# A fused convolution-attention, causal attention and expert block: second-norm transposes placed at the end of their slot, the keys' remainder and the projection placed ahead of the diagonals, the first convolution scores placed ahead in their slot, and the convolution sum in 64-token tiles

## The reference, cut to what matters

```python
# 1. convolution attention (per batch, x is 64 x 256, th and ph are 32 x 256)
f = einsum('ci,cj->ij', th, ph)            # th = Wt x + bt, ph = Wp x + bp
a = softmax(f, axis=-1)
x = Wo (a g) + bo + x                      # g = Wg x + bg
# 2. causal attention, 4 heads of 16
t = tokens(x)                              # 256 x 64
t = t + attn(layernorm(t)) @ W_proj
# 3. mixture of 8 experts, all evaluated
u = layernorm(t)
w = softmax(mean_over_batches(u) @ Wr + br)
y_e = relu(bn(relu(bn(u @ W1_e)) @ W2_e)) @ Wo_e + bo_e
out = t + sum_e w_e * y_e
```

## Time and profile before

| | us |
|---|---|
| median of 3 runs | 104.9 |
| those three runs | 104.9, 105.04, 100.9 |
| the profiled execution | 101.54 |
| its span, first to last instruction | 99.7 |
| busy in the span: PE, DVE, ACT, POOL | 81.4, 44.2, 41.8, 15.9 |
| mean granted TensorE clock in the span | 0.914 of full |

### The profile page before, as it was taken

One profiled execution on the slowest core, in us unless ns is written; L12 is line 12 of the kernel. 1 busy time (PEld: TensorE's weight loads), 2 busy tenths in 40 slices (PEclk: granted clock), 3 DMA queues, 4 the chain that ended last, 5 costly groups with the idle time before them and its releaser, 6 DMA issues.

```text
span 99.7 us, 1342 instructions
## 1 busy us (share of the span) xinstructions
PE 81.4 (82%) x482; PEld 51.6 (52%) x482; DVE 44.2 (44%) x138; ACT 41.8 (42%) x81; POOL 15.9 (16%) x27
## 2 busy tenths in 40 slices
PE   5998798586988897909978098897599899799990
PEld 1376697475566475606755055472344347464350
DVE  1027589867694049250861503804212400409751
ACT  2234623355024717613076030158546675663420
POOL 2000214520282012020400201501310200000000
PEclk9999999999669999997599755569999999999999
DMA  1960000000000000000000000000000000000003
GB/s 35 297 262 2 0 0 0 0 7 0 3 0 0 0 0 7 0 0 0 0 0 0 0 0 0 0 3 0 7 0 0 0 0 0 0 0 7 0 0 105
DMA packets 960, 1.83 MB, mean 18 GB/s; under 512 B 119, under 2 KB 568, under 8 KB 954
## 3 DMA queue, kind: packets, MB, share of 16 engines
q1 hardware_dynamic: 732, 1.54, 4.7%
q10 hardware_dynamic: 222, 0.21, 0.8%
HBM read 1.48 MB, written 0.26 MB: 18 GB/s over the span
## 4 chain that ended last, share of the span: by engine, by line
PE 63%; DVE 13%; issue 9%; ACT 8%; POOL 4%; ACTq 0%; POOLq 0%
PE A L615 21%; PE PR L615 18%; PE M L615 10%; PE Q L615 10%; ACT qk_tmp L374 3%; DVE m L525 3%; DVE ln_xs L512 2%; POOL ln_rs L334 2%; PE Q L635 2%; ACT h L384 2%; ACT p L429 2%; DVE th_s L463 1%; DVE ph_s L463 1%; DVE ln_st L501 1%; POOL diag L291 1%
## 5 line engine op out<-in xcount | busy, mean ns | idle before, releaser
L384 ACT ACTIVATE h<-PR,bn_c,bn_s 128x512 f32<-128x512 f32 (+1 forms) x16 | 10.2, 666 | 5.5 <-PE PR L615 5.2
L291 POOL TENSOR_TENSOR diag<-neg_ident,m 128x256 fp32r<-128x256 f32 (+1 forms) x8 | 6.6, 826 | 28.4 <-DVE m L551 17.9
L334 POOL TENSOR_TENSOR ln_rs<-ln_var,half 128x2 f32<-128x2 f32 x8 | 5.6, 700 | 32.0 <-DVE ln_var L506 32.0
L374 ACT ACTIVATE qk_tmp<-PR 128x512 fp32r<-128x512 f32 x8 | 4.3, 594 | 10.8 <-PE PR L615 10.8
L615 PE MATMUL PR<-h,pack_ffn 128*64 128x256 f32 (+2 forms) x32 | 8.6, 446 | 0.0
L551 DVE TENSOR_REDUCE m<-A 128x4 f32<-128x512 f32 x4 | 2.8, 690 | 12.4 <-PE A L615 12.4
L635 PE MATMUL Q<-pack_ident,ln_xs 128*128 128x128 f32 x8 | 1.9, 327 | 6.8 <-DVE ln_xs L512 6.8
L429 ACT ACTIVATE p<-A 128x512 f32<-128x512 f32 (+1 forms) x8 | 6.0, 808 | 2.9 <-PE A L615 2.9
L512 DVE TENSOR_SCALAR ln_xs<-t,ln_mv,ln_rs 128x128 f32<-128x128 f32 x16 | 5.1, 361 | 4.3 <-POOL ln_rs L334 4.3
L604 DVE TENSOR_TENSOR h<-h,A 128x512 f32<-128x512 f32 x8 | 5.1, 684 | 3.9 <-PE A L615 2.8
L615 PE MATMUL PR<-x2T,pack_ffn 64*128 64x512 f32 (+1 forms) x16 | 6.0, 654 | 0.4 <-ACT h L384 0.3
(11 more groups left out here) (118 smaller groups left out, 148.6 us busy)
## 6 DMA issues: line engine op xcount, KB each, us to landing
pack_ffn<-in_pack_ffn_dram SPq DMA_DIRECT2D x1, 712.0 KB, 6.1
pack_attn<-in_pack_attn_dram SPq DMA_DIRECT2D x1, 276.0 KB, 4.0
out_dram<-o_sb SPq DMA_DIRECT2D x2, 128.0 KB, 1.7
x<-in_x_dram SPq DMA_DIRECT2D x1, 195.0 KB
pack_conv<-in_pack_conv_dram ACTq DMA_DIRECT2D x1, 130.5 KB
pack_ident<-in_pack_ident_dram ACTq DMA_DIRECT2D x1, 70.0 KB, 3.6
x<-in_x_dram SPq DMA_DIRECT2D x1, 65.0 KB
```

Source lines behind the costliest of these rows:

```text
L291: return engine.tensor_tensor(out, neg_ident[:, :].unsqueeze(1).to_broadcast([P, n, P]), m.unsqueeze(2).to_broadcast([P, n, P]), ALU.mult)
L334: pool.tensor_tensor(ln[i]["rs"][b][:, :], ln[i]["var"][b][:, :], half[:, 0:NB], ALU.pow).then_inc(ln[i]["s_pow"], 1)
L374: return act.activation(out, in_, ACT.Copy)
L384: act.activation(out, bank, ACT.Relu, bias=bn_c[:, i, q:q + 1], scale=bn_s[:, i, q:q + 1]).then_inc(relu_ok, 1)
```

## The change

Four edits to the order and one to the form of a product:

1. Step 10 (second norm's transposes on PE, the `x2T` copy on ACT) leaves the head of both lists and stands behind 8.2, 12.1 and 12.2, in the same slot.
2. The keys' remainder is step 5.5 now, one slot later, behind step 7; its ACT copy is step 5.6. On ACT the copy of the values (step 5) now comes ahead of it.
3. Step 9 (projection) stands ahead of 7.1 on PE.
4. Step 1 stands ahead of steps 3 and 0 on PE, and ahead of 3 on DVE (9 and 9.1 move within DVE's list too, without a change of order there, since slot 10 holds nothing else that they pass).
5. Each product of step 3 is made as two, with 64 tokens each, whose results lie on partitions 0 to 63 and 64 to 127.

The table of slots now names each fractional step.

```diff
--- before.py
+++ after.py
@@ -262,7 +262,8 @@
 
         FILL = {"loads": 10, "router": 2}
         CONV_STEPS = 4
-        ATTN_SLOT = {4: 4, 5: 5, 6: 7, 7: 8, 8: 9, 9: 10, 10: 11}
+        ATTN_SLOT = {4: 4, 5: 5, 5.1: 5, 5.2: 5, 5.5: 6, 5.6: 6, 6: 7, 6.1: 7, 6.2: 7, 7: 8, 7.1: 8, 8: 9, 8.1: 9, 8.2: 9, 9: 10,
+                     9.1: 10, 10: 11}
         FFN_SLOT = {11.0: 13, 11.1: 14, 12.0: 15, 12.1: 15, 12.2: 15, 12.3: 16,
                     13.0: 16, 13.1: 16, 14.0: 16, 14.1: 16, 14.2: 17, 14.3: 17}
         FFN_PIECES = {11.0: (0, 0, (0, 1)), 11.1: (0, 0, (2, 3)),
@@ -276,7 +277,7 @@
                 return FFN_SLOT[step] if b == 0 else None
             if step < CONV_STEPS:
                 return int(step) + b
-            return ATTN_SLOT[int(step)] + 2 * b
+            return ATTN_SLOT[step] + 2 * b
 
         def schedule(*order):
             for slot in range(SLOTS):
@@ -388,7 +389,7 @@
                 act.wait_ge(ln[i]["s_T"], b + 1)
                 copy(out, bank[:, 0:N]).then_inc(ln[i]["s_TT"], 1)
 
-            for step, b in schedule(10, 8, 12.0, 0, 2, 0.1, 5.1, 5.2, 8.2, 12.1, 12.2, 5.3, 5, 11.0, 7, 11.1, 12.3,
+            for step, b in schedule(8, 12.0, 0, 2, 0.1, 5.1, 5.2, 8.2, 12.1, 12.2, 5, 10, 11.0, 5.6, 7, 11.1, 12.3,
                                     13.0, 13.1, 14.0, 14.1, 4, 14.2, 14.3):
                 if step == 0:
                     act.wait_ge(f_ps, b + 1)
@@ -418,7 +419,7 @@
                         act.wait_ge(k_ok, b - 1)
                     act.wait_ge(k_ps, b + 1)
                     copy(qk_tmp[b][:, 1, :], PR[1][:, :]).then_inc(k_rnd, 1)
-                if step == 5.3:
+                if step == 5.6:
                     act.wait_ge(k_split, b + 1)
                     copy(k_s[b][:, :, :].rearrange("p g n -> p (g n)"), PR[1][:, :]).then_inc(k_ok, 1)
                 if step == 7:
@@ -513,7 +514,7 @@
                                     l["mv"][b][:, n, 0:1], l["rs"][b][:, n:n + 1],
                                     ALU.subtract, ALU.mult).then_inc(l["s_xs"], 1)
 
-            for step, b in schedule(9, 9.1, 6, 8.1, 6.1, 6.2, 3, 1, 0, 5.1, 3.1, 8, 7, 2):
+            for step, b in schedule(6, 8.1, 6.1, 6.2, 1, 3, 0, 5.1, 3.1, 9, 9.1, 8, 7, 2):
                 if step == 0:
 
                     v.wait_ge(f_rnd, b + 1)
@@ -659,8 +660,8 @@
                     last = mm(bank, w2[:, q, :], h1[:, q, columns_of(s)])
                 last.then_inc(layer_ps, 1)
 
-            for step, b in schedule(10, 8, 12.0, 6, 8.1, 12.1, 3, 0, 2, 2.1, 5.1, 5, 8.2, 12.2, 5.2, 11.0, 7, 7.1, 9, 11.1, 12.3,
-                                    13.0, 13.1, 14.0, 14.1, 1, 0.1, 4, 14.2, 14.3):
+            for step, b in schedule(8, 12.0, 6, 8.1, 12.1, 1, 3, 0, 2, 2.1, 5.1, 5, 8.2, 12.2, 10, 11.0, 7, 5.5, 9, 7.1, 11.1, 12.3,
+                                    13.0, 13.1, 14.0, 14.1, 0.1, 4, 14.2, 14.3):
                 if step == 0:
 
                     pe.wait_ge(x_in[min(b, 1)], 16)
@@ -714,8 +715,10 @@
                     pe.wait_ge(vx_ok, b + 1)
                     for i in range(NB):
                         for j in range(NB):
-                            last = mm(pv1[b][:, i, :], p1[b][:, j, i * P:(i + 1) * P], vx[b][:, j, 0:C + 1],
-                                      start=(j == 0), stop=(j == NB - 1))
+                            for t in range(2):
+                                tokens = slice(i * P + t * C, i * P + (t + 1) * C)
+                                last = mm(pv1[b][t * C:(t + 1) * C, i, :], p1[b][:, j, tokens], vx[b][:, j, 0:C + 1],
+                                          start=(j == 0), stop=(j == NB - 1))
                     last.then_inc(pv1_ps, 1)
                 if step == 4:
                     if b > 0:
@@ -745,7 +748,7 @@
                                       start=(g == 0), stop=(g == 1))
                             if g == 1:
                                 last.then_inc((q_ps, k_ps)[i], 1)
-                if step == 5.2:
+                if step == 5.5:
                     if b == 0:
                         pe.wait_ge(v_const, 5)
                     pe.wait_ge(k_rnd, b + 1)
```

## The result

| | before | after |
|---|---|---|
| median of 4 runs, us | 102.9 | 97.48 |
| lowest and highest | 100.46, 105.04 | 96.06, 102.85 |
| profiled execution, its span | 101.54, 99.7 | 96.08, 94.3 |
| mean granted clock in it | 0.914 | 0.909 |

The ratio is 0.952, with an interval of 0.941 to 0.963: the changed kernel is faster by 5%. The forecast was 93.0, in a range of 90.5 to 95 of its own and 90.5 to 98.0 with its rivals. The measured time lies in the upper part, which only a rival had put in.

A forecast was written before the change was run, and what follows sets the result against it. Bound by PE's waits for the second norm's transposes, low clock and a convolution loop over PE, ACT and DVE. 101.54 - 10.9 + 0.3 = 90.9, plus 1.7 clock and 0.4 tiles: 93.0 us, own range 90.5 to 95, with rivals to 98.0.

The forecast's parts named there:

- the convolution loses over 3 us: Convolution part: a loss above 3 us there was named as showing the prediction wrong.
- Batch 0's scores near 26.6: Start of attention: batch 0's attention scores were to start at 26.6 us, against 25.07 before, a loss of 1.5.
- batch 2's sum near 21: Convolution part: batch 2's sum was to start at 21.15 us, against 18.97 before, 2.2 us lost.
- The pairs: Attention part: slot pairs between successive batches' scores, the last to the first second layer, at 7.6, 8.7, 8.9 and 10.0 us.
- The wait for `x2T`: First expert layer: ACT's `x2T` copy stands directly ahead, uncovered, leaving PE idle 0.45 us.
- batch 0's pair: From batch 0's attention scores to batch 1's: 3.15 + 2.17 + 1.51 + 0.8 = 7.6 us, the maximum ending 3.15 in.
- the changed kernel is no denser there: Just before batch 0's scores: the first low-clock stretch, 3.40 us of busy PE, was kept at a price of 1.7.
- +0.1 a sum: Convolution sums in 64-token tiles: each was to cost 0.1 us more, 0.4 for four.
- The clock falls as often as before: Rival: first low stretch in the convolution, others later, all three kept; 98.0 us, chance 0.20.
- The wait moves to ACT: Rival: with a late remainder, `k_s` delays each exponential by 0.6 and PE waits; 94.7 to 95 us, chance 0.08.
- The convolution order costs nothing: Rival: PE takes projections in another order or DVE's earlier maximum repays them; 91.5 us, 90 without low stretch, chance 0.09.
- slower: Rival: clock falls in the convolution until the expert layers; 37 us of low clock gives 103.6 us, chance 0.04.

The follow-up runs named there:

- the filled kernel: The changed kernel with products on zeros ahead of the convolution scores' wait for `f_split`: median 92.7 us, ratio 0.903 to the kernel before.
- the last kernel: The changed kernel with edits 4 and 3 undone and products on zeros in seven places: median 87.21 us of 8 runs.
- that of 88.23: Profiled execution of the changed kernel with edit 4 undone: 88.23 us, lowest of four runs with median 93.57.

## Why the prediction was right, and where it was off

**Right in its range, but not by its own signs.** The change was forecast as a gain through edit 1, and it is one. But the prediction named as a sign of being wrong that the convolution loses over 3 us, and it loses 6.2 (25.62 against 19.46). Batch 0's scores near 26.6, batch 2's sum near 21 and a mean clock of 0.97 did not come either (31.16, 25.74, 0.909). That the time lies within 98.0 is in part luck: the range was widened for three low stretches where they were before, and one of another cause and place, as long as all three, took their room.

**Right: what edit 1 does.** The three waits are gone, and the low clock behind them: from 26 us on it is 1.00 in the profiled execution. The pairs were forecast at 7.6, 8.7, 8.9 and 10.0 and came out at 8.29, 8.70, 8.77 and 10.17. The wait for `x2T` ahead of the first expert layer was put at 0.45 and is 0.72; those for exponentials at 0.3 and 0.7 are 0.20 and 0.58. The end behind the first second layer is 27.2 long, 0.2 more than before (forecast 0.3).

**Off: batch 0's pair,** 7.6 forecast, 8.29 measured. The step that failed put the end of the maximum 3.15 after the scores. PE waits 0.81 for it, and the transposed scores start at 34.88, 3.72 after 31.16. DVE was late: it waited 0.81 for POOL's root of batch 1's first norm, and both maxima (0.68 and 1.21 long) came behind that norm's writing:

```profile
32.50 0.60 DVE L513 TENSOR_SCALAR ln_xs<-t,ln_mv,ln_rs 128x128 f32<-128x128 f32 x2 [0.81 <-POOL ln_rs L335]
33.02 0.68 DVE L552 TENSOR_REDUCE m<-A 128x4 f32<-128x512 f32 x1
```

**Off: the clock.** The prediction kept one low stretch of 3.4 us at 1.7. It came as 17 us. The step that failed is "the changed kernel is no denser there": it kept the old stretch at its old length, where the new loop is thinner. PE waits 1.15 for `f_split` ahead of the first scores and is busy for 1.92 us of the loop's first 3.07 at full clock, against 2.79 of 3.07 in the kernel before. The first row is of the kernel before, the second of the kernel before with edit 4 alone, each from its first projections on:

```profile
5.61:8.68 3.07, 2.79 (x16) 2.23 (x15) 0.87 (x2) 1.68 (x4) 0.00 (x0) 1.00 0.37 147
5.22:8.29 3.07, 1.92 (x12) 1.62 (x11) 1.23 (x5) 1.09 (x3) 0.00 (x0) 1.00 0.46 187
```

The length of the loop at full clock came out (21.0 from the first projections to batch 0's scores forecast, 20.85 with the loop's idle time filled), in part by luck: the forecast had sums of 0.95, and with tiles the sum of batch 2 comes at 14.95 in place of 15.54; behind it the filled kernel has the 0.43 for POOL's diagonal. The terms written out from 21.15 to 26.6 add up to 3.94 only; the sum of batch 2 and what follows it up to the queries and keys (18.97 to 20.54, 1.57) are in the 26.6, but not named. At 1.2 GHz PE's projections in the loop take 1.91 in place of 1.03, and the slots grow from 3.07, 3.07 and 4.0 to 4.04, 4.19 and 5.53. That makes 4.6 us at batch 0's scores (31.16 against 26.6); the pairs add 0.7, the end takes back 0.1, and 1.7 and 0.4 had been set aside for the stretch and the tiles: 4.6 + 0.7 - 0.1 - 2.1 = 3.1, which is 96.08 - 93.0.

**Off: edit 5.** Priced at +0.1 a sum, in bounds of -0.25 to +0.23; it is -0.3 at full clock and -0.5 at 1.2 GHz, outside the bounds. The rows that bounded it move 128 or 256 columns a product, so they were no floor for one that moves 65. What did bound the sum is not shown by a run of its own; the rows of the weight loads (PEld) point to loading the stationary columns, which fills 0.97 of its 1.11 us before and 0.58 of 0.69 after:

```profile
12.16 0.97 PEld L615 LDWEIGHTS A<-vx,p 128*128 128x128 f32 x8 [0.53 <-DVE m L525]
```

```profile
25.71 0.58 PEld L616 LDWEIGHTS A<-vx,p 128*64 128x64 f32 x16 [0.68 <-issue]
```

The Trainium skill (TensorEngine Tiling (Array Packing), Key Properties) says that a change of tiling mode drains TensorE; no cost of it shows here: with two changes of tile shape each, the sums are shorter, not longer.

**Missed: edits 3 and 4 are losses.** The prediction listed edit 3 with the gain. Its own sum put the projection's 0.6 ahead of the exponentials of each pair, but it never priced the pair without the edit, which it took for a cover of `k_s`. It cost 1.7 us: a step put ahead of the diagonals delays the exponentials by about its whole length, while behind them the projection cost nothing that shows. Edit 4 was named a cost of 2.2 at batch 2's sum; at batch 0's scores it is 2.6 at full clock and 7.4 with its clock in the profiled executions.

**The rivals.** "The clock falls as often as before" came out in its outcome (mean clock 0.909 and 0.914) and partly in its mechanism: the first stretch came in the convolution part, with the loop as its cause, but no others came later in the profiled execution. "The wait moves to ACT" did not come: at batches 1 and 2 `k_s` ends at 45.39 and 54.11, and ACT then idles 0.42 and 0.48 for PE before the exponentials (45.81, 54.59). "The convolution order costs nothing" is refuted by the ratio of 1.097 with edit 4 alone. That kernel is also what "slower" described, a clock that falls in the convolution and stays low far into the attention (to 38.4). In the changed kernel it came back at 26; the two runs of ten at 0.81 may be cases in which it did not, but neither was profiled.

## What to carry to other kernels

A move that lets the busiest engine go on while others work is worth about twice (here 5.9 of waits and 5.5 of clock) if the wait it removes was also what let TensorE's clock fall; ask of each edit what it does to TensorE's idle time in its own stretch, also where the edit's direct cost is small. Put what does not feed the next exponentials behind the products that do. And take a bundle of edits apart: here one of five gave about twice the gain of all, and another took 4 us (medians) to 8 us (lowest runs) of it back.

## What the runs showed of the hardware

**The clock decides in both directions.** The same instructions in the same order gave 96.06 at a mean clock of 0.91 and 102.72 at 0.81. Work on zeros in idle time made kernels faster: 101.77 to 97.93, and a ratio to the kernel before of 0.952 to 0.903 (97.48 and 92.7).

**The clock fell behind short waits.** In the changed kernel it fell at about 8.3 us behind a single wait of 1.15 us, in the kernel with edit 4 alone behind two of 1.15, and with those waits filled it did not fall there. In these loops it then stayed low for 17 to 30 us (17 in the changed kernel, 27 with edit 4 alone, 30 without the tiles), although in the changed kernel PE was busy for 16.0 of those 17.0 us.

**The clock field does not show a clock that is low from the start.** In the profiled execution of the last kernel (95.27; the two high runs have the same mean clock) the page gives a mean clock of 0.98, yet the first projections take 2.07 us in place of 1.13, and sums and projections keep the lengths of 1.2 GHz until about 24 us:

```profile
5.97 2.07 PE L616 MATMUL Q<-x,pack_conv 65*128 65x256 f32 x4
...
15.67 1.14 PE L616 MATMUL A<-vx,p 128*64 128x65 f32 x16
...
25.15 0.69 PE L616 MATMUL A<-vx,p 128*64 128x65 f32 x16
```

```profile
PEclk9999999999999999999999999999999966999999
```

The granted clock stands at full in the row all that while. The profiled execution of the changed kernel without edit 3 (98.81, mean clock 0.98) is the same: its first projections take 2.08, and its sums 1.14 and 1.13 up to 27. The ten products on zeros at the start of each kernel also run at first as at 1.2 GHz, under a field of 1.00: in the execution of 95.27 all ten take 4.45 us (0.43 apart), in that of 88.23 they take 3.64. So for the stretch up to the first change in the record the lengths of products tell the clock, not the field. Runs of the kernel before near 110 to 116 at 0.87 to 0.92, and one of edit 4 alone (113.19 at 0.97), may be of that kind; none of them was profiled. So a comparison at one mean clock, as used above, holds only where the start was at full clock, which the time itself has to tell.
